# Two-layer AdaLN/FFN kernel: last chunks of the attention in another order, and spare TensorE products

## The reference, cut to what matters

```
x = x + msa(layernorm(x))            # 4096 rows of 128; 16 heads of 8, over the 32 rows of one batch
h = layernorm(x)
logits = h @ gate_w + gate_b         # 8 experts, one is chosen for each row (argmax)
x = x + w2[e] @ gelu(w1[e] @ h)      # 128 -> 512 -> 128, e the row's expert
```

## Time and profile before

| what | value |
|---|---|
| median of 3 runs | 617.62 us |
| the profiled execution | 619.02 us, its span 617.3 us |
| PE busy | 504.6 us, 82% of the span |
| DVE busy | 363.5 us, 59% |
| ACT busy | 283.4 us, 46% |
| POOL busy | 154.4 us, 25% |
| granted TensorE clock, mean | 0.942 of 2.4 GHz |

### The profile page before, as it was taken

One profiled execution on the slowest core, in us unless ns is written; L12 is line 12 of the kernel. 1 busy time (PEld: TensorE's weight loads), 2 busy tenths in 40 slices (PEclk: granted clock), 3 DMA queues, 4 the chain that ended last, 5 costly groups with the idle time before them and its releaser, 6 DMA issues. The chain is left out here.

```text
span 617.3 us, 35472 instructions
## 1 busy us (share of the span) xinstructions
PE 504.6 (82%) x15374; PEld 414.1 (67%) x15374; DVE 363.5 (59%) x1161; ACT 283.4 (46%) x691; POOL 154.4 (25%) x258
## 2 busy tenths in 40 slices
PE   0888988888986979799999768689888861599995
PEld 0777887877874654566665568567666650499995
DVE  4655555555553257566666448458899977155552
ACT  5221212221212864355456335678667731377772
POOL 2111111111114600000000030143466637055553
PEclk9899999999997988999999989999899965599998
DMA  8060000000000007594230010000011103233330
GB/s 277 2 222 0 0 0 0 0 0 0 0 0 2 1 2 150 127 333 80 69 87 1 0 57 17 2 5 1 19 37 53 40 29 109 83 86 105 108 104 22
DMA packets 22655, 34.39 MB, mean 56 GB/s; under 512 B 3616, under 2 KB 15909, under 8 KB 22216
## 3 DMA queue, kind: packets, MB, share of 16 engines
q1 hardware_dynamic: 19824, 27.23, 16.0%
q0 software_dynamic: 2784, 6.56, 3.0%
HBM read 25.98 MB, written 8.26 MB: 55 GB/s over the span
## 5 line engine op out<-in xcount | busy, mean ns | idle before, releaser
L230 PE MATMUL ps_u<-v_cur,buf_b 128*32 128x32 f32 x7936 | 76.4, 198 | 6.3 <-DVE v_cur L287 1.4
L230 PEld LDWEIGHTS ps_u<-v_cur,buf_b 128*32 128x32 f32 x7936 | 72.7, 109 | 11.6 <-DVE v_cur L287 10.9
L215 PE MATMUL ps_v<-buf_a,u_pad 128*32 128x128 f32 x1984 | 62.9, 281 | 7.2 <-issue 5.8
L215 PEld LDWEIGHTS ps_v<-buf_a,u_pad 128*32 128x32 f32 x1984 | 54.3, 113 | 10.8 <-issue 9.1
L585 PE MATMUL ps_h<-buf_c,up 128*128 128x512 f32 x96 | 51.4, 642 | 0.4 <-DVE buf_c L777 0.4
L1700 POOL DMA_INDIRECT out<-yb,token_i x39 | 38.5, 986 | 49.7 <-DVE resid L1802 48.6
L195 ACT ACTIVATE over<-u_diff 128x32 f32<-128x32 f32 x31 | 7.1, 230 | 94.2 <-POOL u_diff L175 94.2
L179 POOL TENSOR_TENSOR u_hist<-inv_u,r_sum 128x16 f32 x62 | 13.7, 221 | 141.9 <-DVE inv_u L294 141.9
L1723 PE MATMUL m_h<-xT,w_near 128*128 128x128 f32 x312 | 43.1, 283 | 0.1
L1733 PE MATMUL m_y<-w,hid_t 128*128 x312 | 42.1, 279 | 0.1
L1276 POOL TENSOR_TENSOR vb<-vn,row_mask 128x1024 f32<-128x1024 f32 x16 | 30.3, 1892 | 44.8 <-ACT vn L1458 41.5
(11 more groups left out here) (305 smaller groups left out, 1132.8 us busy)
## 6 DMA issues: line engine op xcount, KB each, us to landing
cw_b<-cw_d SPq DMA_DIRECT2D x16, 512.0 KB, 7.7
xt<-sorted_x SPq DMA_DIRECT2D x39, 136.0 KB, 2.2
w<-in_w SPq DMA_DIRECT2D x2, 2048.0 KB, 16.9
buf_a<-in_x SPq DMA_DIRECT2D x4, 512.0 KB, 5.8
buf_b<-in_x_t SPq DMA_DIRECT2D x4, 512.0 KB, 7.0
buf_d<-in_x_nt SPq DMA_DIRECT2D x1, 2048.0 KB, 10.5
sorted_x<-nobody SPq DMA_DIRECT2D x1, 1088.0 KB, 4.8
out<-yb,token_i POOLq DMA_INDIRECT x39, 2.4
```

Source lines behind the costliest of these rows:

```text
L215: last = mm(ps_v[h][32 * j:32 * j + 32, 0:D], u_pad[:, h, j, 32 * i4:32 * i4 + 32], K[:, g * D:(g + 1) * D], start=i4 == 0, stop=i4 == TI - 1)
L230: last = mm(rows_u[h][32 * q:32 * q + 32, g, :], KT[:, b * N:(b + 1) * N], v_cur[:, h, k:k + 1].broadcast_to([P, WIDE]), start=True, stop= ...
```

## The change

Four edits. DVE's chunk loop runs `scales` after `spread` in place of before `add`, and 10 of the small operations of `moments`, `scales` and `choose` are written as SCALAR_TENSOR_TENSOR with a multiplication by 1.0 (`both`) in place of TENSOR_TENSOR. Chunk 15 and what follows are written in another order on DVE, PE and ACT. POOL sends the blocks of the fifth pair (two of them are left) after `mix` of chunk 14 in place of 15. PE gets products whose result nobody reads: 4, 3, 3, 2, 20 and 40 at the end of the attention, and 16 at the head of the experts.

```diff
-                pool.wait_ge(o_mm, NC)
-                for t in range(sent, G):
+                pool.wait_ge(o_mm, NC - 1)
+                for t in range(sent, 2 * S.first[GROUPS - 3]):
+                    send(t)
+                pool.wait_ge(o_mm, NC)
+                for t in range(2 * S.first[GROUPS - 3], G):
                     send(t)
...
+                def spare(n):
+                    for k in range(n):
+                        mm(ps_qk[:, 0, 0:P], ident[:], w_qkv[:, 0, :], start=True, stop=True)
+
+                pe.wait_ge(qk_out, NC)
+                spare(4)
+                turn(NC - 1, 1)
+                turn_output(NC - 2, 0)
                 pe.wait_ge(sub_done, NC)
                 rank(NC // 2)
-                turn_output(NC - 2, 0)
-                turn(NC - 1, 1)
+                spare(3)
+                mix(NC - 1, 1)
                 project_output(NC - 2, 0)
-                mix(NC - 1, 1)
+                spare(3)
                 turn_output(NC - 1, 1)
+                spare(2)
                 project_output(NC - 1, 1)
                 rank(NC // 2 + 1)
+                spare(20)
                 rank(NC // 2 + 2)
+                spare(40)
...
+                turned(NC - 1)
                 output(NC - 2)
                 inverse_root(GROUPS - 2)
-                turned(NC - 1)
...
+                def both(out, a, b, op):
+                    return stt(out, a, 1.0, b, ALU.mult, op)
...
-                    c.step(tt(gap[:, gs], rstd[:, gs], rstd[:, gs], ALU.mult))
+                    c.step(both(gap[:, gs], rstd[:, gs], rstd[:, gs], ALU.mult))
...
-                for i in range(NC):
+                for i in range(NC - 1):
                     below_most(i)
                     if i >= 6 and i % 2 == 0:
                         place(i // 2 - 3)
-                    if i >= 4 and i % 2 == 0:
-                        scales(i // 2 - 2)
...
                     if i >= 2:
                         spread(i - 2)
+                    if i >= 4 and i % 2 == 0:
+                        scales(i // 2 - 2)
                     if i >= 3 and i % 2 == 1:
                         moments(i // 2 - 1)
+                below_most(NC - 1)
+                add(NC - 3)
+                over_sum(NC - 2)
+                choose(GROUPS - 3)
+                spread(NC - 3)
+                moments(GROUPS - 2)
                 place(GROUPS - 3)
+                over_sum(NC - 1)
+                add(NC - 2)
                 scales(GROUPS - 2)
                 choose(GROUPS - 2)
-                add(NC - 2)
-                over_sum(NC - 1)
+                add(NC - 1)
+                place(GROUPS - 2)
                 spread(NC - 2)
-                add(NC - 1)
                 spread(NC - 1)
                 moments(GROUPS - 1)
-                place(GROUPS - 2)
                 scales(GROUPS - 1)
...
+                for k in range(16):
+                    mm(ps_y[0][:, 0:P], ident[:], ident[:], start=True, stop=True)
                 turn(0)
                 turn(1)
                 up(0)
```

More of the change, by code:

```diff
@@ L1551, in moments @@
                     dve.wait_ge(own, c.n)
-                    c.step(tt(gap[:, gs], six[:, gs, 1], six[:, gs, 4], ALU.subtract))
-                    tt(total[:, gs], six[:, gs, 1], six[:, gs, 4], ALU.add).then_inc(own, 1)
+                    c.step(both(gap[:, gs], six[:, gs, 1], six[:, gs, 4], ALU.subtract))
+                    both(total[:, gs], six[:, gs, 1], six[:, gs, 4], ALU.add).then_inc(own, 1)
                     c.n = c.n + 1
-                    c.step(tt(var[:, gs], six[:, gs, 2], six[:, gs, 5], ALU.add))
+                    c.step(both(var[:, gs], six[:, gs, 2], six[:, gs, 5], ALU.add))
                     c.step(stt(gap[:, gs], gap[:, gs], 0.25, gap[:, gs], ALU.mult, ALU.mult))
@@ L1561, in scales @@
                     dve.wait_ge(rooted, n + 1)
-                    c.step(tt(gap[:, gs], rstd[:, gs], rstd[:, gs], ALU.mult))
+                    c.step(both(gap[:, gs], rstd[:, gs], rstd[:, gs], ALU.mult))
                     c.step(stt(gap[:, gs], var[:, gs], LN_EPS, gap[:, gs], ALU.add, ALU.mult))
                     c.step(ts(gap[:, gs], gap[:, gs], -0.5, 1.5, ALU.mult, ALU.add))
-                    c.step(tt(rows[:, gs, ROOT], rstd[:, gs], gap[:, gs], ALU.mult))
+                    c.step(both(rows[:, gs, ROOT], rstd[:, gs], gap[:, gs], ALU.mult))
                     stt(rows[:, gs, SHIFT], total[:, gs], -0.5, rows[:, gs, ROOT], ALU.mult, ALU.mult).then_inc(row_ends, 1)
@@ L1572, in choose @@
                         dve.wait_ge(slots_done, IDLE + n + 1)
-                    c.step(tt(logits[:, gs, :], rows[:, gs, D:WIDE], rows[:, gs, ROOT:ROOT + 1].broadcast_to(wide), ALU.mult))
-                    c.step(tt(logits[:, gs, :], logits[:, gs, :], gate_bias[:, None, :].broadcast_to(wide), ALU.add))
+                    c.step(both(logits[:, gs, :], rows[:, gs, D:WIDE], rows[:, gs, ROOT:ROOT + 1].broadcast_to(wide), ALU.mult))
+                    c.step(both(logits[:, gs, :], logits[:, gs, :], gate_bias[:, None, :].broadcast_to(wide), ALU.add))
                     c.step(v.tensor_reduce(top[:, gs], logits[:, gs, :], AX.X, ALU.max))
-                    c.step(tt(eq[:, gs, :], logits[:, gs, :], top[:, gs, None].broadcast_to(wide), ALU.is_equal))
-                    c.step(tt(eq[:, gs, :], eq[:, gs, :], prefer[:, None, :].broadcast_to(wide), ALU.mult))
+                    c.step(both(eq[:, gs, :], logits[:, gs, :], top[:, gs, None].broadcast_to(wide), ALU.is_equal))
+                    c.step(both(eq[:, gs, :], eq[:, gs, :], prefer[:, None, :].broadcast_to(wide), ALU.mult))
                     c.step(v.tensor_reduce(top[:, gs], eq[:, gs, :], AX.X, ALU.max))
-                    tt(hot[:], eq[:, gs, :], top[:, gs, None].broadcast_to(wide), ALU.is_equal).then_inc(hot_done, 1)
+                    both(hot[:], eq[:, gs, :], top[:, gs, None].broadcast_to(wide), ALU.is_equal).then_inc(hot_done, 1)
                 def place(n):
```

## The result

The changed kernel takes 629.31 us (median of 6 runs, 627.28 to 633.21); the kernel before 618.08 us (6 runs, 614.55 to 621.54). The ratio is 1.0184, with a 95% interval of 1.0136 to 1.0232. Slower by over 1%, as forecast; the prediction had 628 and a range of 613 to 633.

The account below looks back on a forecast made before the run. It took DVE to bound the chunk loop and PE the experts. Loop 7.0, clock 2.6, end -0.8 and head 1.5 gave +10.3 us on the profiled 619.02, so 629.3, or 628 for the median; range 613 to 633.

Parts of the forecast that it names:

- `scales` behind `spread`: Chunk loop: `on` ends earlier, the second `vb` stalls `choose` by 1.7 us, a pair takes 0.9 us more.
- The loop term: Chunks 4 to 15: 2.5 us more in the first pair and 0.9 in each of five others, 7.0 us.
- The clock term: Chunk loop: PE's longer stand before `rank` gives three clock falls where there was one, 2.6 us more.
- its own case: The forecast's case: `choose` stalled and 0 to 4 clock falls in the loop, 623 to 630 us, chance 0.47.
- Rival 3: Chunk loop: the clock falls in every pair, 3.9 us above the forecast, 632 us; chance 0.17.
- The signs that the prediction named for the loop: Subtractions of equal parity 14.3 to 15 us apart; PE idle over 3 us before `rank`.
- PE is the last: End of the attention: PE's 40 products after the last `rank` end last, so 0.8 us less, though POOL wins 4.
- The head: Head of the experts: 16 products delay the first real one 4.0 us, the clock returns 2.5; 1.5 us more.
- `both`: Small DVE operations of `moments`, `scales` and `choose`: the rewritten form costs 0 and frees nothing from `vb`.
- Rival 4: Chunk loop: `both` frees DVE from `vb`, every pair 11.6 to 12 us, 606 us; chance 0.02.
- Rival 1: Chunk loop: the second `vb` misses `choose`, a pair takes 12.7 us, about 611 us; chance 0.11.

Follow-up runs that it names:

- kernel 1: The kernel before with one edit, `scales` behind `spread` in DVE's chunk loop; 632.43 us, ratio 1.0191.
- kernel 4: The kernel before with `scales` behind `spread` and 10 unread PE products ahead of each `rank` in the loop; 624.21 us, ratio 1.0078.
- kernel 6: The kernel before with `scales` behind `spread` and POOL's `vb` for only the first half of a chunk's batches; 615.91 us, ratio 0.9934.
- kernel 5: The changed kernel with 10 unread PE products ahead of each `rank` of the loop; 623.42 us, ratio 1.0087.
- kernel 8: The changed kernel with the old chunk loop and without the 16 products at the head of the experts; 619.9 us, ratio 1.0007.
- kernel 3: The kernel before with only the small operations written as SCALAR_TENSOR_TENSOR (`both`); 619.93 us, ratio 0.9963.
- kernel 10: The kernel before with `scales` moved ahead of `place` in the even chunks; 617.97 us, ratio 0.9979.

## Why the prediction was right

**Direction and mechanism.** The step "`scales` behind `spread`" said that `on` comes earlier, that the second `vb` then meets `choose`, and that PE's stand grows at `rank`. Kernels 1, 4 and 6 and the trace show each of these. At the full clock of kernel 4 the times of that step are nearly met too: counted from the first operation of the even chunk, `on` ends at 4.35 us (forecast 4.1 to 4.7), `choose` starts at 8.8 us (forecast 8.9 to 9.2), the second `vb` at 9.15 (8.9 to 9.4), and `hot` is ready at 11.8 (12.0 to 12.4).

**The loop term was too large.** It put 0.9 us on a pair and 2.5 on the first. Measured at full clock: 0.4 to 0.5 (kernels 4 and 5), and 1.6 on the first pair in the changed kernel (13.15 against 11.51, no fall in either), so 5 x 0.45 + 1.6 = 3.9 us in place of 7.0. Too large was the stall in `choose`: 1.46 us, not 1.7. POOL's second `vb` (it waited 0.64 us for `mix`) started behind the second of `choose`'s operations; the third, a TENSOR_REDUCE with one input, ran its normal 0.19 us beside it, and only the fourth waited. And `hot` was ready earlier than forecast.

**The clock term was too small.** It took three falls at 1.3 us, and its own case allowed 0 to 4. There were five, one in each pair behind the first, at 1.2 to 2.6 us (the pairs against 14.1): the whole is 8.4 - 1.3 = 7.1 us in place of 2.6. The row from which the price came, chunk 8 of the kernel before, had PE slack around it. In the changed loop PE goes without a wait from `rank` to the next `mix`, and DVE waits for it. Rival 3, one fall in every pair, came true in its mechanism; its 632 is not reached because the loop term is smaller. The two errors nearly cancel: 9.6 forecast, 11.2 measured. The signs that the prediction named for the loop say the same: its pairs of 14.3 to 15 us became 15.3 to 16.7, and PE's stand before `rank` was over 3 us only once (3.32), then 2.86 four times.

**The end: the failed sentence is "PE is the last".** It gave -0.8 us. The block end follows POOL's last send, by 6.4 us to DVE's first copy, of which the loads are only 3.6 to 3.9 (changed kernel, PE's first product after its own last one: 3.9; kernel 8, DVE's first copy after PE's last product: 3.6). I had put all 6.4 into the loads. So POOL's 3.1 us counted in full, and the 40 products, which ended 2.7 us behind POOL, held nothing up.

**The head** was right in both parts against the kernel before: 4.0 us forecast for the 16 and 3.9 measured (12.0 against 8.1 us), 2.5 forecast back and 2.6 measured; 1.3 in place of 1.5. Against the six other kernels with the old end the 16 products cost more, 1.4 to 3.1 us (16.1 against 13.0 to 14.7). One reason was off: the clock was still high when the 16 products began, fell under them and rose again, so that they took 5.3 us and not the 5.5 that I had for a start at the low clock.

**`both`** cost nothing and freed nothing, as two rows and the stall in a SCALAR_TENSOR_TENSOR had said. Rival 4 is out (kernel 3: 0.9963). So is, for operations of this size, the half rate that the Trainium skill states (Vector Engine (DVE) Microarchitecture Reference, section 7): the 32-wide operations of `choose` take 0.19 us in either form.

**Rival 1**, that `vb` misses `choose`, did not come, and its price of 12.7 us a pair is open. With a `vb` of half the length a pair takes 12.9 us, but that edit shortens PE's path too; in kernel 10, where behind chunk 6 no `vb` meets `scales`, `choose` or `place`, the last three pairs take 13.7.

**The sum.** That 628 lies so near to 629.31 is in part luck. In the profiled executions the loop was forecast 1.6 us too short (9.6 against 11.2), the end and the head together 2.6 us too long (+0.7 against -1.9), and 2.0 us of the measured 11.5 lie ahead of all changed code.

## What to carry to other kernels

In a loop that one engine bounds, look at its small operations that take ten times too long, and at what else ends in that moment; then ask where the other engine's work will lie after the move, not only what the move frees. A stand of TensorE of 2.9 us in every pair cost more through the clock than the old one of 2.2 us, which mostly passed. Spare products paid only in such a wait of every pair (experiments 4 and 5): at the head of a stage they delayed the first tile by more than the clock gave back.

## What the runs showed of the hardware that was not expected

- From POOL's last indirect send (its end) to DVE's first operation of the next block it is 6.42 to 6.44 us in 13 of the 14 profiled kernels, whatever the other engines did. The exception is the kernel without the 16 products, where PE ended 4.4 us after POOL (8.0 us).
- PE's clock fell in every pair of the changed loop behind the first, after stands of 3.32 us (once) and 2.86 us (four times) between `mix` and `rank`; the old loop's stands of 2.2 us, between `scores` and `turn_output`, mostly passed.
- PE can fall into gaps of 0.5 to 1.1 us at each instruction with nothing to wait for by the profile, in runs of unread products and in `values` once the loop is tighter.
- Not only operations with two SBUF inputs stand for `vb`. In chunk 6 of kernel 10 a CAST of `place` with a single input took 1.65 us in place of 0.17 and ended with `vb`, while a TENSOR_REDUCE just before it ran 0.19 us beside `vb`:

```profile
436.87 0.19 DVE L1586 TENSOR_REDUCE slot<-eq 128x4 f32<-128x32 f32 x1
437.09 1.65 DVE L1587 CAST slot_i<-slot 128x4 int32<-128x4 f32 x1
436.83 1.89 POOL L1276 TENSOR_TENSOR vb<-vn,row_mask 128x1024 f32<-128x1024 f32 x1 [3.92 <-ACT vn L1458]
```
